# A gated delta-rule layer on one core: second value products ahead of the key rows, query sums two slots later

## The reference

```
qkvz = x @ W_qkvz                            # per key head: q, k, two v, two z
q, k, v = silu(causal_conv1d(q, k, v))       # 4 taps
q, k = l2norm(q) / sqrt(128), l2norm(k)
# per chunk of 64 tokens, g the running sum of the log decay in the chunk
A = -(beta * k @ k.T) * exp(g_i - g_j)       # strictly lower triangle
T = inverse(I - A)                           # row by row in the reference
v' = T @ (beta * v) - (T @ (beta * k * exp(g))) @ state
out = (q @ state) * exp(g) + ((q @ k.T) * exp(g_i - g_j)) @ v'
state = state * exp(g_last) + (k * exp(g_last - g)).T @ v'
core = rmsnorm(out * silu(z)) * norm_w
y = core @ W_out                             # summed over the heads
```

## Time and profile before

| | |
|---|---|
| median of three runs | 5820.58 us |
| the profiled execution | 5815.34 us |
| its span, first to last instruction | 5813.2 us |
| TensorE matmuls busy, mean granted clock | 5127.7 us (88%), 0.948 |
| VectorE, ScalarE, GpSimd busy | 3511.4 (60%), 3049.9 (52%), 1064.8 (18%) |
| chain that ended last | PE 64%, DVE 10%, issue 9%, ACT 8%, SP's queue 5%, DMA 3% |

### The profile page before, as it was taken

One profiled execution on the slowest core, in us unless ns is written; L12 is line 12 of the kernel. 1 busy time (PEld: TensorE's weight loads), 2 busy tenths in 40 slices (PEclk: granted clock), 3 DMA queues, 4 the chain that ended last, 5 costly groups with the idle time before them and its releaser, 6 DMA issues.

```text
span 5813.2 us, 140368 instructions
## 1 busy us (share of the span) xinstructions
PE 5127.7 (88%) x50224; PEld 3593.3 (62%) x50224; DVE 3511.4 (60%) x6423; ACT 3049.9 (52%) x7910; POOL 1064.8 (18%) x1064
## 2 busy tenths in 40 slices
PE   3899999999779999999978999999997899999998
PEld 2566666666556666666645666666664666666666
DVE  6466666666446666666645656666664666666665
ACT  2455555555345555555525555555552555555554
POOL 0021221112112111221211221212220112221122
PEclk9899999999889999999989999999998999999999
DMA  1122222221122221222112222222211221222211
GB/s 66 47 56 48 50 55 52 56 58 41 38 53 57 52 57 41 54 56 52 41 38 58 56 54 52 56 48 50 54 33 56 56 58 41 54 56 52 58 41 37
DMA packets 685902, 296.25 MB, mean 51 GB/s; under 512 B 598976, under 2 KB 642112, under 8 KB 675648
## 3 DMA queue, kind: packets, MB, share of 16 engines
q1 hardware_dynamic: 685120, 286.09, 20.4%
HBM read 213.55 MB, written 59.78 MB: 47 GB/s over the span
## 4 chain that ended last, share of the span: by engine, by line
PE 64%; DVE 10%; issue 9%; ACT 8%; SPq 5%; DMA 3%; DVEq 0%; POOL 0%; ACTq 0%; POOLq 0%
PE pj L587 10%; PE dsb L721 8%; PE ms L642 6%; PE ms L598 4%; PE pot L679 4%; ACT arena L853 4%; SPq L409 4%; PE pj L582 4%; PE pot L650 4%; DVE cy L1132 4%; PE dsb L693 3%; PE pod L662 3%; PE pod L705 3%; PE ms L611 2%; PE ms L626 2%
## 5 line engine op out<-in xcount | busy, mean ns | idle before, releaser
L587 PE MATMUL pj<-xnT,wt 128*128 128x512 f32 x2048 | 1041.2, 638 | 101.6 <-ACT arena L853 59.3
L1132 DVE SCALAR_TENSOR_TENSOR cy<-xpad,cw,cy 128x1024 f32<-128x1024 f32 x768 | 1059.5, 1386 | 32.5 <-ACT cy L873 22.9
L1371 POOL TENSOR_TENSOR rout<-rin,expo 128x2 f32<-128x2 f32 x512 | 366.7, 716 | 2809.6 <-DVE rin L1267 2809.6
L721 PE MATMUL dsb<-wo,yT 128*128 128x256 f32 x2048 | 617.1, 426 | 104.3 <-issue 100.0
L587 PEld LDWEIGHTS pj<-xnT,wt 128*128 128x128 f32 x2048 | 371.2, 199 | 534.5 <-issue 377.3
L1365 POOL TENSOR_TENSOR sdec<-st,gel 128x512 f32<-128x512 f32 x384 | 402.2, 1048 | 1120.9 <-DVE st L1256 935.5
L872 ACT ACTIVATE xpad<-pj 128x512 f32<-128x512 f32 x512 | 302.8, 591 | 578.1 <-PE pj L587 577.7
L931 ACT ACTIVATE yT<-dsb 128x256 f32<-128x256 f32 x512 | 196.7, 384 | 714.0 <-PE dsb L712 712.8
L721 PEld LDWEIGHTS dsb<-wo,yT 128*128 128x128 f32 x2048 | 370.7, 202 | 226.1 <-issue 187.7
L582 PE MATMUL pj<-wt,xnT 128*128 128x256 f32 x2048 | 509.1, 392 | 0.0
L1246 DVE SCALAR_TENSOR_TENSOR rr<-pot,nge,arena 128x128 f32<-128x128 f32 x896 | 271.2, 344 | 352.1 <-PE pot L650 350.6
(11 more groups left out here) (163 smaller groups left out, 8755.4 us busy)
## 6 DMA issues: line engine op xcount, KB each, us to landing
qge<-ge_rows SPq DMA_DIRECT2D x64, 1024.0 KB, 7.1
wt<-in_L_attn_W_qkvz SPq DMA_DIRECT2D x64, 768.0 KB, 4.4
gb<-g_rows SPq DMA_DIRECT2D x128, 256.0 KB, 4.1
a_d<-at SPq DMA_DIRECT2D x64, 512.0 KB, 2.6
wo<-in_L_attn_W_out SPq DMA_DIRECT2D x64, 256.0 KB, 2.7
x_d<-xpair SPq DMA_DIRECT2D x128, 128.0 KB, 1.7
ap_<-a_d SPq DMA_DIRECT2D x512, 16.0 KB, 1.8
dd<-x_d SPq DMA_DIRECT2D x512, 16.0 KB, 1.8
```

Of the source, the lines that this page charges most:

```text
L587: last = mm(pj[n % 2][:, :], wt[:, k, col:col + DH], batch(xnT, k, i), start=(k == 0), stop=(k == KD - 1))
L721: last = mm(dsb[:, 0, GRP * DH:GRP * DH + D], yT[:, h, :], wo[:, p, h, :], start=(h == 0), stop=(h == GRP - 1))
L1132: stt(y, x[:, :, tap:tap + SEQ], cw[:, kind, tap:tap + 1], y, ALU.mult, ALU.add).then_inc(S["conv"], 1)
L1371: tt(rout[:, :], rin[:, :], expo[:, 0, 0:GRP], ALU.pow).then_inc(S["routs"], 1)
```

## The change

Four edits, all to the place of work:

- In the ring both `v1` fills (second values) stand ahead of the key rows, and the two `kt` fills are apart: `v1` in slots 13 and 14, the first `kt` in 14, the second in 19, ahead of `fixpoint`. Before, both `kt` stood in slot 13 and both `v1` in 14.
- TensorE's `square_sums(g, 1)` goes from slot 11 to 13. `chunk_squares(g, p, 1)` stays in 11 and is first there.
- VectorE's `decayed_squares(g, p, 0)`, the key products with the decay, goes from slot 8 to 9. Between the two stand `residual`, `mean_square` and `accumulate` of chunk 3.
- VectorE's `query_eps` goes from slot 11 to 15.

```diff
-        ring = [("k", 0), ("k", 1), ("z", 0), ("q", 0), ("q", 1), ("v0", 0), ("v0", 1), ("kt", 0), ("kt", 1),
-                ("v1", 0), ("v1", 1), ("z", 1), ("z", 2), ("z", 3), ("vt", 0), ("vt", 1), ("vt", 2), ("vt", 3)]
+        ring = [("k", 0), ("k", 1), ("z", 0), ("q", 0), ("q", 1), ("v0", 0), ("v0", 1), ("v1", 0), ("v1", 1),
+                ("kt", 0), ("z", 1), ("z", 2), ("kt", 1), ("z", 3), ("vt", 0), ("vt", 1), ("vt", 2), ("vt", 3)]
...
                 if s == 11:
+                    chunk_squares(g, p, 1)
+                if s == 13:
                     square_sums(g, 1)
-                    chunk_squares(g, p, 1)
-                for n, at_s in enumerate((1, 2, 4, 5, 5, 8, 10, 13, 13, 14, 14, 16, 17, 20, 22, 22, 23, 23)):
+                for n, at_s in enumerate((1, 2, 4, 5, 5, 8, 10, 13, 14, 14, 16, 17, 19, 20, 22, 22, 23, 23)):
...
                     coefficients(g, p)
                     scale_decay(g)
+                if s == 9:
                     decayed_squares(g, p, 0)
-                if s == 11:
-                    query_eps(g, p)
...
                     turn_inverse(g)
+                    query_eps(g, p)
                     decayed_squares(g, p, 1)
```

## The result

The changed kernel takes 6000.19 us (median of 4 runs, 5978.32 to 6010.19) against 5827.09 for the kernel before beside it. The ratio is 1.0299, 95% interval 1.0257 to 1.0341: slower by 3.0%. The profiled execution has a span of 5994.9 us against 5813.2, and a mean granted clock of 0.939 against 0.948.

What follows compares the result with a forecast made beforehand. TensorE was taken as the bound, except that VectorE's inversion chain sets L626. Order +95 us, half clock -105 us and then 1.25 us a pass back, net +65 us on 5820.6: 5885 us, range 5790 to 5970.

Steps and rivals of the forecast that it cites:

- The order: The four edits at full clock: L626 1.03 us later, 0.55 us added behind it, +1.58 us a pass, +95 us.
- `solve`'s new wait: TensorE at `solve` of chunk 4: a new 2.0 us wait for the residual behind VectorE's taps.
- the bank's wait: TensorE's 0.87 us wait at L587 for ScalarE to empty a bank of key rows: it goes.
- the turned copy: `turn_inverse` (L1229) on VectorE, the inverted blocks turned ahead of L626: 1.03 us later.
- the working: The prediction's step-by-step timing of one woven pass at full clock; L626 1.03 us later, +1.58 us a pass in all.
- Key rows behind L626: Second half of the key rows moves behind L626, where TensorE is dense: +0.55 us a pass.
- The clock: Half clock between first key products and L626: 1.25 us a pass instead of 1.75; outcomes bounded from -10 to +157 us.
- the low clock meets the longer chain: Rival: half clock in most passes while L598 and L587 stand ahead of `update`; +157 us, 5978 us, chance 0.15.
- the pass at 0.91: Kernel before, first key products to L626 at granted clock 0.91: 37.49 us, against 34.70 at 1.00.
- the rival's bound of 2.79 us: Half-clock cost ahead of L626 if every woven pass paid like the 0.91 pass: 2.79 us a pass, 167 us.
- The faster rival: VectorE's inversion keeps pace, not held by `update_state` of chunk 4; L626 0.71 us earlier, 5735 us, chance 0.11.

Runs made afterwards that it cites:

- e1: Changed kernel with three added 256-column products nobody reads, on TensorE in slot 12 where it waits for chunk 4's residual; ratio 1.0286.
- e5: Changed kernel with inversion row 7, `join_halves` and `turn_inverse` moved ahead of `update_state` of chunk 4 on VectorE; 5800.41 us, ratio 0.9967.
- e10: Changed kernel with the query sums, `square_sums(g, 1)`, in slot 14 instead of 13; 5898.91 us, ratio 1.0144.
- e4: Kernel before with only the change's new ring order and its slots; 5859.98 us, ratio 1.0071.
- e12: e7 with the ring and slots of the change added; 5747.97 us, ratio 0.9884.
- e2: Kernel before with only `decayed_squares(g, p, 0)` moved to slot 9; ratio 1.0197.
- e9: e2 with four added 256-column products on TensorE ahead of L598, where it idles; ratio 0.9997.
- e3: Kernel before with only `square_sums(g, 1)` in slot 13 and `query_eps` in slot 15; 5860.45 us, ratio 1.0084.
- e7: Kernel before with L611 ahead of L598 in slot 11, `query_eps` in slot 15 and `turn_inverse` in slot 14; 5665.06 us, ratio 0.9716.
- e8: Kernel before with two added 256-column products on TensorE ahead of L598 in slot 11, where it waits for the squares; ratio 0.9986.
- e11: Kernel before with L611 ahead of L598 in slot 11 and `query_eps` in slot 15; 5690.4 us, ratio 0.9788.

## Why the prediction was wrong

*The order.* This was right step by step, and the sum nearly so. `solve` of chunk 4 starts at 17.03 (17.06 forecast), L611 waits 1.40 us for `silu` (1.4), `solve`'s new wait is 2.01 us (2.0), and the bank's wait is gone. In e1's pass at full clock the turned copy is at 28.94 (29.09) and L626 at 35.48 (35.7 forecast, from 34.70). Over all passes at full clock the order costs 0.65 us where the working had 1.03. That the inversion is held by `update_state` of chunk 4 is shown by e5 and e10.

*Key rows behind L626.* The forecast was +0.55 us; the rest of the pass is 0.57 longer in the changed kernel, 0.87 in e4 and 0.74 in e12.

*The clock: the step that failed.* The prediction says "I take 1.25 us a pass" for half clock ahead of L626, less than the 1.75 that it read for the kernel before. Measured by the same reading it is 39.01 - 35.48 = 3.5 us a pass (by the means of all passes at full clock 3.5 after and 1.6 before, so the 1.75, taken from one pass, was a little high). Of the 2.56 us by which the mean stretch grew, 0.65 are the order at full clock and the other 1.9 come with the clock; this is a split of a measured sum and no check of it. With the 0.57 behind L626 it is 3.13 us a pass, 188 us over 60 passes, where the spans differ by 181.7. With 3.5 in the place of 1.25 the working would have given 5821 + 95 - 105 + 210 = 6021. I had the mechanism, a slow L587 ahead of `update`, and wrote its worst case down as a rival, "the low clock meets the longer chain", at 5978 us and 0.15. That was the nearest.

Two things were too small in that term. The amount: half clock rose from 4.2 to 6.7 us a pass, where a term under 1.75 meant less of it. And the price: the pass at 0.91, from which the rival's bound of 2.79 us came, had the same 6.7 us of half clock as the mean pass has now, and it costs 3.5. From a granted clock of 1.00 to 0.95 the stretch of e1 grows by 1.91 us, that of the kernel before by 1.25. The traces show why at the place itself: the 3.0 us by which L598, L587 and `update` are slower reach the turned copy whole, because `update_state` stands in the middle of the inversion.

*Why so low.* I read the new order as a quiet place less: sums and key products apart. What counted was idleness beside the one-column products: 2.01 us of waiting, a short `solve` and the sums. With the wait filled half clock is 4.6 us (e1), with the sums taken from behind it 3.0 (e10), with both 6.7. And I added edits up in which each takes a wait away and makes a later one longer. e2 shows this most plainly: 0.76 us of wait was removed, the idleness ahead of L598 went up by 1.19, 2% was lost, and nearly all of it was given back by e9's filler. e3's part, which I took for the larger share, is less than half of e2's.

*The faster rival* needed `update` to end in time for the inversion. e5 got there by moving the inversion instead, and is faster than the kernel before by 0.3%. That does not make the other edits good: the kernel before with the same move was not run, and e12 shows the new ring as a loss of 83 us on e7.

*What is left open.* No run shows why the wait at the loop's turn grows when products are added, why the three parts together cost less than their sum, or how far the changed kernel would be from the one before if both ran at full clock throughout; the 0.65 us rest on e1, which has added products.

## What to carry to other kernels

A wait taken away ahead of another wait may only lengthen that one, and here a longer idle stretch of TensorE beside one-column matmuls brought half clock to what followed: price a reordering by where the idleness gathers, not by the waits that go. Compare stretches at the same granted clock before you say what the order costs. When an engine idles inside a chain that another waits for, first ask whether the rest of the chain can go ahead of the wait; here that one move was worth some 200 us. Fill a wait with the work next in line that is ready (here by swapping two neighbours, with `query_eps` out of the way, 2.1%), not with work made up for it.

## What the runs showed that I had not expected

The record of the granted clock has half clock during L598 in 56 of 60 passes with 2.4 to 2.5 us of idleness ahead of it (e2), in 22 with 1.28 us (before), and in at most 4 where most or all of that wait is filled, by added products (e8, e9) or by the products next in line (e7, e11). From a granted clock of 0.95 to 0.91 the mean stretch grew by 1.35 us in the kernel before, by 1.41 in the changed one, and by 1.55 in e5, although TensorE no longer waits for `dd` in its woven passes: taking the chain out of the way did not make half clock cheap. What moved most between the kernels was its amount, from 2.1 to 7.3 us a pass. Three kernels with a few added products lost, where the loop turns, 1.7 to 2.1 us more at each of 24 waits (100.0 us in all before, 141.7 to 149.8 with them).
